# First attention's scores as fp32 matmuls in 32x64 blocks, V whole, Y in 64x32 blocks, in a decoder layer on one core

## The reference

```python
qkv = x @ W_attn; q, k, v = split(qkv)          # 16 heads of 8
att = einsum('bhid,bhjd->bhij', q, k) / sqrt(8)
att = where(causal, att, -inf)
att = polymax(att)        # (x*x + 1)/1000 for x > 0, (1 - 0.01*x)/1000 for -100 <= x <= 0, else 0
y = einsum('bhij,bhjd->bhid', att, v) @ W_proj
x = layernorm(x + y)
q, k, v = x @ WQ, ctx @ WK, ctx @ WV             # 16 heads of 64, softmax over 64 keys
x = layernorm(x + (softmax(q k / 8) v) @ WO + bO)
p = softmax(x @ router_w.T + router_b)           # 16 experts, the 6 best, their shares renormed
x = layernorm(x + sum_e gate[:, e] * (x @ expert_w[e]))   # within the reference: out / acc + tiny terms
```

## Time and profile before

| | |
|---|---|
| median of 3 runs | 1042.84 us (1041.07 to 1043.26) |
| the profiled execution | 1043.48 us, span 1041.4 us |
| PE busy | 993.9 us, 95% |
| DVE busy | 978.6 us, 94% |
| ACT busy | 762.2 us, 73% |
| POOL busy | 395.1 us, 38% |
| mean granted clock of TensorE | 0.986 of full speed |
| DMA | 25.16 MB, 24 GB/s over the span |

### The profile page before, as it was taken

The page is one execution under the profiler, slowest core; times in us unless marked ns, Lnnn a source line. Parts: engine busy times, 40 slices in busy tenths (PEclk is TensorE's granted clock), DMA queues, the critical chain, the costliest instruction groups (busy, mean ns, idle before and its releaser), DMA issues.

```text
span 1041.4 us, 44466 instructions
## 1 busy us (share of the span) xinstructions
PE 993.9 (95%) x16856; PEld 868.0 (83%) x16856; DVE 978.6 (94%) x3176; ACT 762.2 (73%) x1606; POOL 395.1 (38%) x681
## 2 busy tenths in 40 slices
...
DMA packets 29577, 25.16 MB, mean 24 GB/s; under 512 B 2528, under 2 KB 24544, under 8 KB 29536
## 3 DMA queue, kind: packets, MB, share of 16 engines
...
...
## 4 chain that ended last, share of the span: by engine, by line
DVE 39%; issue 26%; PE 24%; POOL 4%; ACT 4%; DVEq 2%; DMA 0%; ACTq 0%; POOLq 0%; SPq 0%
PE ps L420 22%; DVE sums L860 15%; DVE allowed L824 4%; DVE ps L831 3%; DVE stats L777 3%; DVE p L805 2%; ACT x L733 2%; POOL rstd L985 2%; DVE p L837 1%; DVE residual L860 1%; DVE left L896 1%; PE ps L571 1%; DVE mv L783 1%; PE ps L548 1%; DVE residual L945 1%
## 5 line engine op out<-in xcount | busy, mean ns | idle before, releaser
L860 DVE SCALAR_TENSOR_TENSOR sums<-ps,gate,sums 128x128 f32<-128x128 f32 x896 | 241.7, 345 | 1.5 <-ACT x L733 1.2
L992 POOL TENSOR_TENSOR p<-p,rowinv 128x1024 f32<-128x1024 f32 x64 | 121.9, 1904 | 36.0 <-DVE rowinv L813 36.0
L982 POOL TENSOR_TENSOR rstd<-mv,ln_eps_tile 128x2 f32<-128x2 f32 x96 | 18.7, 195 | 295.3 <-DVE mv L783 292.0
L420 PE MATMUL ps<-wo_sb,oT 128*128 128x128 f32 x1024 | 122.7, 278 | 2.9 <-issue 0.5
L420 PEld LDWEIGHTS ps<-wo_sb,oT 128*128 128x128 f32 x1024 | 116.7, 192 | 6.7 <-issue 6.2
L733 ACT ACTIVATE x<-residual,shift,rstd 128x128 f32<-128x128 f32 x192 | 83.9, 487 | 39.9 <-POOL shift L987 39.7
L420 PE MATMUL ps<-ex_hi,x2T_hi 128*128 128x512 f32 x256 | 106.7, 417 | 5.3 <-DVE p L805 2.7
L635 ACT ACTIVATE relu<-ps 128x512 f32<-128x512 f32 x128 | 75.9, 596 | 45.2 <-PE ps L420 44.5
L420 PE MATMUL ps<-ex_lo,x2T_hi 128*128 128x512 f32 x256 | 102.8, 402 | 0.0
L420 PE MATMUL ps<-ex_hi,x2T_lo 128*128 128x512 f32 x256 | 102.6, 401 | 0.0
L824 DVE SCALAR_TENSOR_TENSOR allowed<-ps,const 128x512 f32<-128x512 f32 x128 | 87.6, 686 | 8.5 <-ACT relu L635 5.7
...
## 6 DMA issues: line engine op xcount, KB each, us to landing
...
```

Of the source, the lines that this page charges most:

```text
L420: return pe.matmul(o, l, r, start=start, stop=stop)
L860: done = V.scalar_tensor_tensor(after, ps(f"FF{4 * r + q}")[:, C * e:C * e + C], gate[:, r, 4 * q + e:4 * q + e + 1], before, ALU.mult, AL ...
L992: G.tensor_tensor(weights, weights, rowinv[:, r].unsqueeze(2).broadcast_to([P, H, T]), ALU.mult).then_inc(p2_ready, 1)
```

## The change

- PART becomes 32, PARTS 4, NV 4: s1 is one call a tile, of 16 fp32 matmuls. Each takes 32 rows (four heads of 8) and 64 columns (the keys of one sequence) of the array and moves 256 columns (the queries of one sequence, masked for four heads). Four row groups write four banks, and two sequences the two halves of the partitions. Neither keys nor queries are split: kT is one plain copy of K, qm four scaled and masked copies of Q, both on ACT. keys_lo and queries_lo are gone from DVE.
- V is two fp32 matmuls of 128 columns on the whole array, and one copy on ACT puts each head's 8 columns into a place of 32 columns, zero elsewhere.
- Y is 64 fp32 matmuls in 64x32 blocks (64 keys x 32 columns of output), each moving 64 columns, four accumulating; the two sequences go to two banks, so Y takes a pair. move_y reads both.
- x_columns fetches one of the two copies of x in HBM that it fetched before.
- All orders, banks and lags are new: Q and K run four tiles ahead instead of one, FF one behind instead of two. The loop's turns are 1 to 27 (27 turns as before). S2_0, AC0, S2_1 stand together, and S1, AC1. Three waits are written out where the order no longer gives them.

```diff
-PARTS = 2
-NV = J // PARTS
-PART = P // PARTS
+PART = 32
+PARTS = P // PART
+NV = PART // HD
+VALUE_PAD = PART - HD
...
+    ("PT0a", "B7", 1), ("FF0", "B0", -1), ("K2_0", "B5", 2), ("K2_1", "B2", 2), ("K2_3", "B3", 2),
+    ("FF1", "B4", -1), ("FF4", "B5", -1), ("X1T", "B6", 2), ("V", "B3", 3), ("FF5", "B2", -1),
+    ("K2_2", "B7", 2), ("Q2_2", "B1", 2), ("Q2_0", "B6", 2), ("FF2", "B7", -1), ("FF6", "B5", -1),
+    ("PT1a", "B3", 1), ("PT0b", "B0", 1), ("Q2_1", "B6", 2), ("FF3", "B1", -1), ("FF7", "B0", -1),
+    ("Q2_3", "B6", 2), ("K", "B7", 4), ("Q", "B2", 4), ("S2_0", "P2", 2), ("AC0", "P3", 1),
+    ("S2_1", "P0", 2), ("PT1b", "B3", 1), ("S1_0", "B2", 4), ("Y", "P3", 3), ("X2T", "B4", 0),
+    ("V2_0", "B5", 2), ("S1_1", "B3", 4), ("PR", "B7", 3), ("S1_2", "B6", 4), ("LG", "B4", 0),
+    ("S1_3", "B1", 4), ("AC1", "P2", 1), ("V2_2", "B7", 2), ("V2_3", "B0", 2), ("V2_1", "B4", 2),
+    ("WO0", "B5", 1), ("WO1", "", 1), ("heads0", "P0", None), ("heads1", "P1", None), ("heads2", "P2", None),
...
     "ACT": """
+        mPT0a@1 mV2_1@1 mK2_0@2 square3@3 norm1@2 mK2_3@2 mK2_1@2 x1_hi@2 base3@-1 mK2_2@2 mQ2_0@2 mV@3 mQ2_2@2 norm2@0 mPT0b@1
+        mQ2_1@2 mQ2_3@2 kK@4 queries@4 mPT1a@1 mAC0@1 mPT1b@1 exp0@2 mY@3 mX2T@0 norm3@-1 mV2_0@2 exp1@2 relu0@4 mAC1@1 relu1@4
+        square0@4 logit_exp@0 mV2_2@2 square1@4 relu2@4 square2@4 relu3@4 mV2_3@2
     "DVE": """
+        gate7@-1 attended@0 gate8@-1 gate9@-1 var1@2 gate10@-1 pieces2@3 stats2@0 allow3@3 gate11@-1 p1_2@3 gate12@-1 pieces3@3
+        gate13@-1 row_inv1@1 gate14@-1 p1_3@3 gate15@-1 x1_lo@2 weigh0@-1 var2@0 weigh1@-1 weigh2@-1 weigh3@-1 stats3@-1 row_max0@2
+        less_max0@2 var3@-1 row_max1@2 less_max1@2 projected@3 logits@0 row_sum0@2 gate0@0 row_sum1@2 stats1@3 gate1@0 allow0@4
+        allow1@4 gate2@0 pieces0@4 gate3@0 row_inv0@2 gate4@0 p1_0@4 gate5@0 pieces1@4 gate6@0 p1_1@4 allow2@4
     "POOL": """
+        context_lo@2 bias_x1@1 root1@2 shares1@1 root2@0 next_x_hi@4 next_x_lo@4 root3@-1 x2_hi@0 context_hi@3 shares0@2 x2_lo@0
...
             def v(tile):
+                for r in range(NR):
+                    last = mm(ps("V")[:, C * r:C * r + C], xT[:, P * r:P * r + P], w_attn_sb[:, 2 * C:3 * C])
+                return last
...
+            def s1(tile):
                 wait_emptied(pe, "Q", tile)
                 wait_emptied(pe, "K", tile)
+                for r in range(NR):
+                    for g in range(PARTS):
+                        for s in range(2):
+                            rows, b = slice(PART * g, PART * g + PART), 2 * r + s
+                            done = mm(ps(f"S1_{g}")[64 * s:64 * s + 64, NV * T * r:NV * T * r + NV * T], kT[rows, b], qm[rows, b].rearrange("p v t -> p (v t)"))
+                            if r == NR - 1 and s == 1:
+                                done.then_inc(full[f"S1_{g}"], 1)
...
             def y(tile):
                 wait_emptied(pe, "V", tile)
+                for g in range(PARTS):
+                    wait_emptied(pe, f"S1_{g}", tile)
+                pe.sem_inc(heads_begun, 1)
+                for r in range(NR):
+                    for v in range(NV):
+                        for g in range(PARTS):
+                            for s in range(2):
+                                keys, place = slice(64 * s, 64 * s + 64), VALUE_PAD + PART * (H * r + NV * g + v) - HD * v
+                                last = mm(ps("Y")[PART * g:PART * g + PART, 512 * s + T * r:512 * s + T * r + T], vp[keys, place:place + PART], p1[keys, g, r, v],
+                                          v == 0, v == NV - 1)
...
             def move_keys(tile):
-                copy(kp_hi[:, :, 0], keys, kmask[:, 0:1])
-                copy(kp_hi[:, :, 1], keys, kmask[:, 1:2]).then_inc(k_hi_ready, 1)
+                move("K", tile, kT[:].rearrange("p b t -> p (b t)"), ps("K")[:, 0:TOK])
...
-            def queries_lo(tile):
-            def keys_lo(tile, parity):
```

More of the change, by code:

```diff
@@ L98 @@
[L98 to L101, removed]
+        mV@0 queries@0 kK@0 relu0@0 relu1@0 square0@0 square1@0 relu2@0 square2@0 relu3@0 square3@0 heads_hi2@0 kK@1 heads_hi1@0
@@ L102 @@
+        mV2_0@1 relu0@3 relu1@3 square0@3 mAC1@0 square1@3 relu2@3 square2@3 mV2_2@1 relu3@3 mV2_3@1 mV@3 exp1@1 square3@3 mK2_2@2
+        mV2_1@1 norm1@2 mPT0a@1 mK2_0@2 x1_hi@2 mK2_3@2 mPT0b@1 mK2_1@2 mQ2_0@2 mQ2_2@2 kK@4 mQ2_1@2 mPT1a@1 mQ2_3@2 mV2_0@2 mAC0@1
+        norm2@0 queries@4 mPT1b@1 mY@3 exp0@2 mAC1@1 exp1@2 mV2_2@2 relu0@4 mX2T@0 square0@4 relu1@4 square1@4 relu2@4 logit_exp@0
+        mV2_3@2 square2@4 relu3@4
     """,
     "DVE": """
[L104 removed]
@@ L109 @@
-        allow3@2 pieces3@2 p1_2@2 p1_3@2 attended@0 stats2@0 var2@0 queries_lo@3 less_max0@1 projected@2 stats1@2 logits@0 var1@2
-        row_sum0@1 gate0@0 row_max1@1 row_inv0@1 gate1@0 less_max1@1 gate2@0 x1_lo@2 gate3@0 gate4@0 gate5@0 gate6@0 allow0@3 gate7@0
-        row_sum1@1 gate8@0 gate9@0 gate10@0 gate11@0 pieces0@3 gate12@0 gate13@0 row_inv1@1 gate14@0 allow1@3 gate15@0 p1_0@3
-        pieces1@3 weigh0@0 weigh1@0 p1_1@3 weigh2@0 weigh3@0
+        allow0@0 allow1@0 pieces0@0 pieces1@0 p1_0@0 p1_1@0 allow2@0 allow3@0 pieces2@0 pieces3@0 p1_2@0 p1_3@0 heads_lo1@0
@@ L113 @@
+        p1_0@3 pieces1@3 p1_1@3 row_sum0@1 var1@2 row_inv0@1 allow2@3 allow3@3 pieces2@3 attended@0 p1_2@3 stats2@0 pieces3@3
+        row_sum1@1 x1_lo@2 var2@0 p1_3@3 row_inv1@1 row_max0@2 less_max0@2 row_max1@2 less_max1@2 row_sum0@2 row_sum1@2 allow0@4
+        pieces0@4 logits@0 allow1@4 pieces1@4 gate0@0 row_inv0@2 gate1@0 projected@3 gate2@0 p1_0@4 gate3@0 p1_1@4 gate4@0 gate5@0
+        allow2@4 gate6@0 stats1@3
     """,
     "POOL": """
-        next_x_hi@0 next_x_lo@0 context_hi@0 next_x_hi@1 next_x_lo@1 context_lo@0 root1@0 next_x_hi@2 next_x_lo@2 experts_lo@0
@@ L121 @@
     "SP": """
-        x_rows@-1 context@-1 store@-5 store@-4 store@-3 store@-2 store@-1
+        context@-1 store@-5 store@-4 store@-3 store@-2 store@-1
     """,
     "PE": """
-        WO0@-4 WO1@-4 S2_0@-3 K@-1 Q@-1 Y@-2 V2_3@-3 V2_1@-3 PR@-2 V2_2@-3 X2T@-4 S1_0@-1 S1_1@-1 LG@-4 V@-1 S2_1@-3 K2_3@-2 K2_2@-2
-        X1T@-2 K2_0@-2 K2_1@-2 PT0a@-3 PT0b@-3 Q2_3@-2 Q2_2@-2 Q2_1@-2 FF0@-4 AC0@-3 FF1@-4 FF4@-4 Q2_0@-2 PT1b@-3 PT1a@-3 FF5@-4
-        S1_2@-1 S1_3@-1 FF2@-4 FF6@-4 V2_0@-2 FF7@-4 FF3@-4 AC1@-3 WO0@-3 WO1@-3 V2_3@-2 S2_0@-2 Y@-1 V2_1@-2 PR@-1 V2_2@-2 X2T@-3
```

205 lines of the change are left out of this document (81 added, 124 removed), and 9 rows, old and new, of the table JOBS.

## The result

The changed kernel takes 1057.19 us (median of 4 runs, 1056.21 to 1057.95), the kernel before 1041.95 us beside it (1040.68 to 1043.26): ratio 1.0146, 95% interval 1.0127 to 1.0164. It is slower by 1.5%, where 994 us were forecast. The profiled execution has a span of 1054.4 us, 13.0 more than before.

A forecast was written before the change was run, and what follows sets the result against it. PE and DVE were both taken as full at 30.67 us a turn; PE's savings gave 28.9, new waits 29.3. Over 27 turns -37, head and tail -7, -1 and -4: span 992, plus 2, 994 us; range 980 to 1022.

The forecast's parts named there:

- it isn't the bound any more, and has 1.4 us or more to spend on waits: DVE in the loop: its work falls from 30.1 to 27.5 us a turn, leaving slack for waits.
- S1, V: PE in the loop: S1 goes from 1.80 to 1.03 us with eight blocks at once, V from 0.59 to 0.45.
- The second rival: PE's S1 and Y: only four blocks run at once, S1 +0.89 and Y +0.87 us, 1051 us; chance 0.07.
- The argument from the records 6.7 ns apart: PE's Y: close starts within a round mean the number of blocks limits, not issue; Y stays 1.03 us, cost 0.
- The first rival: PE's Y: pace of issue limits, 13.8 ns a record, +0.87 us a turn, 1019 us; chance 0.10.
- changes of form: PE in the loop: fewer switches between fp32r work and fp32 or block work, -0.3 and -0.2 us a turn.
- the new waits: PE in the loop: waits that the new orders add, taken as 0.4 us a turn in all.
- the four close waits: Loop: FF0 for x2_lo, context_lo ahead of K2_0, FF0's bank behind mV2_3, S2_0 and PR for mQ2_3 and mY; 0.4 us together.
- Head and tail [...] hold five tiles' worth of the same work: 5 x 1.4 = -7: Code outside the loop, 213.3 us before: five tiles each gain the turn's 1.4 us, -7 us in all.
- The -1 for the first scores: Start: the first S1 no longer waits for the splits on DVE (idle 3.58 us for qm_lo), -1 us.
- the tail came out about as said: Tail: weigh0 to weigh3 of tile -2 stand behind the last attended, where DVE sat idle 4.88 us, -4 us.

The follow-up runs named there:

- e_gate: The changed kernel with gate14 and gate15 moved ahead of row_inv1 in DVE's steady order, nothing else moved: 1032.84 us, ratio 0.9908 against the kernel before.

## Why the prediction was wrong

The forecast missed by 63 us: 24 in the loop's turn (30.18 us for 29.3), 7 in the first two turns behind the start, and some 32 in the start and the tail. By WO's starts, 27 turns apart as in the prediction:

```profile
119.60 2.95 PE L422 MATMUL ps<-wo_sb,oT 128*128 128x128 f32 x25
...
940.92 2.95 PE L422 MATMUL ps<-wo_sb,oT 128*128 128x128 f32 x25
```

The stretch between took 821.3 us against 828.1 before (forecast 791); the start is 25.8 us longer (119.60 for 93.83; forecast a few us shorter); from the later WO to the end it is 113.5 for 119.5.

**DVE.** The step that failed in the loop is "it isn't the bound any more, and has 1.4 us or more to spend on waits". Most of the work did leave (28.4 us a turn remain in e_gate, 0.55 of them tall's surplus; forecast 27.5), but the forecast took DVE's operations at their old durations and looked in the new order for semaphores alone. Two durations depend on what POOL does at the same time. 1.34 - 0.18 = 1.16 us of gate15 and 0.55 of tall came back, and PE waited 0.59 us a turn for x1_lo behind gate15. It was there to be seen: the diff moves gate15 from ahead of row_inv1 to behind it, and the row of L910 has a maximum of 1378 ns beside a median of 178. Price: 27 x 0.88 = 24 us of the 63, and e_gate gives back 24.4.

**S1, V.** Right: 1.05 and 0.46 us. Eight 32x64 blocks do work at once, which no row before had shown: S1's 32 records start in four groups of eight, each group within 0.05 us and 0.22 to 0.27 us behind the one before. The second rival, four at once, falls.

**Y.** Mis-sized: +0.39 us a turn, not 0. The argument from the records 6.7 ns apart took a burst for a pace. It holds for the first 32 of the 128 records (0.24 us); the 96 behind take 10.7 ns each, and Y takes 1.42 us, not 1.03. S1 has 32 records in all, each block busy for 0.2 us, and doesn't meet this. The first rival was right in kind and half in size (its bound 13.8 ns). The Trainium skill (page "TensorE: Matmul & The Clock Gate", section "Wait — 56ns, not 53.3ns?") has about 25 ns from start to start as the least, which as an estimate would make 3.2 us. The trace doesn't agree: 10.0 ns a record over the 128.

**Changes of form and waits.** With gate15 out of the way the turn is 29.34 us, Y's 0.39 included; without Y's surplus it would be 28.95, against the forecast 29.3. So the terms for changes of form and for the new waits were together 0.3 us too dear. That e_gate's turn meets the forecast is luck: this error and Y's cancel. Of the four close waits only q2T's shows (0.2 us, in 15 turns here and in 25 of e_gate).

**Start.** "Head and tail [...] hold five tiles' worth of the same work: 5 x 1.4 = -7" is the other step that failed: it put no waits on the new order of the start. The -1 for the first scores came true (9.19 us for 10.56), and the tail came out about as said (-6). The start is 26 us longer. Up to the second WO PE is idle for 36.9 us where it was idle for 16.1, and busy for 82.7 where it was for 77.8. Of the 20.8 us more of idle time, 9.9 are the wait for xT_lo (K@1 ahead of the transposes), 9.0 the arriving instructions (9.8 for 0.8) and 3.0 a wait for cT_lo; the wait for qm_lo (3.6) is gone. Waits overlap, so putting one right gives back less: the first is worth 6.5 us alone, and 2.0, not resolved, on top of e_gate. The instructions come in at one piece for 256 records: the changed kernel has 14252 PE records in 25 turns, 570 a turn, where the kernel before has 14220 in 27, 526, and Y's now come twice as dense. The first three turns between WOs past the start take 34.6, 32.4 and 30.2 us. The runs with half of Y give 12 us, about 4 of them work. The third part is the granted clock: 0.90 and 0.91 in 40:120 of the changed kernel, 1.00 before, and it stands below 1.00 in slices that hold or follow PE's stops (0.83 in 104:112 with the stop of 2.33 us, 0.74 in the next 8 us). Over the first 200 us it is at half speed for 20.5 us, for 6.8 before: 7 us of time at most. The Trainium skill (page "Runtime: NRT & Kernel Launch", section "Instruction fetch mechanics") says that instructions come in 16 KiB blocks and that fetching is hidden behind the pace of issue; the blocks' size agrees (0.03 MB for two), the hiding doesn't: 16 long stops of 19.3 us together, up to 2.33 us at a time.

**What stays open.** With both orders mended and half of Y gone, the fourth turn's WO still starts 15 us later than before (200.6 for 185.3 us). PE is idle for 31.6 of the first 200 us there, for 16.9 before. One more tile is in flight between Q and FF, so part of it is work done earlier; how much is order and how much is still instructions (12.7 us without a reason remain in that run) I didn't separate. That the long waits are for instructions rests on their places, multiples of 256 records apart, on the pieces that move 2.3 to 2.9 us ahead of their ends, and on four runs in which they follow the number of instructions (5.8, 11.6 and 12.7 us with half of Y, 5.2 for 1.3 with Y twice; 17.9 to 24.4 in the ten profiles with a whole Y); no row names them. What they cost in time is known only with the clock's share in it.
